# Applying a mixture-of-experts gate in ScalarE's PSUM eviction instead of in VectorE's combine

## The reference

```
x = x + 0.5 * ffn(layernorm(x))
x = x + attention(layernorm(x))          # score = q k^T / sqrt(hd), no softmax; rope on q and k
x = x + 0.5 * ffn(layernorm(x))

ffn(x):
    logits = x @ router_weight                        # 8 experts
    top_vals, top_idx = top_k(logits, 2)
    scores = softmax(top_vals)                        # the two gates of a token, their sum is 1
    w = zeros(T, 8) with scores at top_idx
    gate, up = even and odd columns of x @ gate_up_proj + bias, clipped at 7
    act  = (up + 1) * gate * sigmoid(1.702 * gate)
    down = act @ down_proj + bias
    out  = sum over experts of w * down
```

## Time and profile before

| | us |
|---|---|
| median of 3 runs | 793.53 (792.43 to 795.62) |
| the profiled execution, its own time | 793.87 |
| its span, first to last instruction | 792.0 |
| PE busy | 606.5 (77%) |
| VectorE busy | 496.9 (63%) |
| POOL busy | 418.2 (53%) |
| ScalarE busy | 312.1 (39%) |
| chain that ended last | PE 58%, VectorE 19%, DMA 7% |

### The profile page before, as it was taken

How to read it: one execution, slowest core, us unless ns; L and a number is a source line. 1 busy time by engine, 2 the same in 40 slices (tenths; PEclk the granted TensorE clock), 3 DMA queues, 4 the chain that set the end, 5 groups by cost and what they waited for, 6 DMA issues and landing times.

```text
span 792.0 us, 13509 instructions
## 1 busy us (share of the span) xinstructions
PE 606.5 (77%) x3716; PEld 511.5 (65%) x3725; DVE 496.9 (63%) x1103; ACT 312.1 (39%) x660; POOL 418.2 (53%) x484
## 2 busy tenths in 40 slices
PE   3656249999999995577777699924899999999800
PEld 2655138888888884355556589913688888888700
DVE  5855945555555552799998268875455555555367
ACT  3445234444444443244445224413444444444300
POOL 2655335777777754177777510002577777776400
PEclk9999999999999998699999779955899999999955
DMA  9566012333333321433331235200233233333189
GB/s 312 195 205 180 1 45 74 94 96 94 97 99 97 94 78 44 144 120 86 115 119 35 92 88 158 94 26 21 73 95 95 93 98 99 93 94 91 49 281 354
DMA packets 43366, 87.47 MB, mean 110 GB/s; under 512 B 7363, under 2 KB 22777, under 8 KB 42820
## 3 DMA queue, kind: packets, MB, share of 16 engines
q1 hardware_dynamic: 20898, 43.30, 16.9%
q0 software_dynamic: 13664, 35.35, 15.0%
q10 hardware_dynamic: 8770, 8.41, 3.1%
HBM read 53.50 MB, written 35.36 MB: 112 GB/s over the span
## 4 chain that ended last, share of the span: by engine, by line
PE 58%; DVE 19%; DMA 7%; issue 6%; POOL 5%; ACT 2%; DVEq 1%; SPq 1%; ACTq 0%; POOLq 0%
PE ps L770 14%; PE ps L771 14%; PE ps L772 14%; PE ps L761 10%; DVE xs L1264 5%; PE ps L765 3%; DMA work<-y_dram 2%; DVE work L1292 2%; DVE work L1291 2%; PE ps L788 2%; DMA xn_dram<-work 2%; POOL up_lo L435 2%; DVE work L1076 2%; DVE bst L1060 1%; DVE work L1192 1%
## 5 line engine op out<-in xcount | busy, mean ns | idle before, releaser
L761 PE MATMUL ps<-cst,work 128*128 128x128 f32 x824 | 137.1, 292 | 77.7 <-DVE work L1076 59.6
L474 POOL DMA_INDIRECT y_dram<-work,sidx x142 | 142.8, 1005 | 83.6 <-issue 49.5
L761 PEld LDWEIGHTS ps<-cst,work 128*128 128x128 f32 x824 | 103.9, 150 | 97.5 <-DVE work L1076 57.4
L466 POOL DMA_INDIRECT work<-xn_dram,gidx x142 | 139.3, 981 | 44.5 <-issue 44.5
L770 PE MATMUL ps<-up_hi,xT_hi 128*128 x284 | 125.6, 442 | 0.8 <-issue 0.8
L771 PE MATMUL ps<-up_lo,xT_hi 128*128 x284 | 113.2, 398 | 0.0
L772 PE MATMUL ps<-up_hi,xT_lo 128*128 x284 | 113.0, 398 | 0.0
L1214 DVE TENSOR_TENSOR xT_lo<-ps,xT_hi 128x512 fp32r<-128x512 f32 x72 | 49.8, 691 | 97.8 <-ACT xT_hi L613 97.8
L1229 DVE TENSOR_SCALAR work<-ps 128x256 f32<-128x256 f32 x142 | 60.3, 425 | 72.5 <-ACT work L627 72.5
L627 ACT ACTIVATE work<-ps 128x256 f32<-128x256 f32 x142 | 54.6, 384 | 111.4 <-PE ps L772 111.4
L635 ACT ACTIVATE work<-ps 128x512 f32<-128x512 f32 x72 | 42.6, 592 | 96.3 <-PE ps L772 96.3
(11 more groups left out here) (149 smaller groups left out, 1407.5 us busy)
## 6 DMA issues: line engine op xcount, KB each, us to landing
work<-y_dram SPq DMA_DIRECT2D x32, 512.0 KB, 3.9
xs<-L_attn_x SPq DMA_DIRECT2D x4, 1024.0 KB, 7.3
work<-L_ffn_gate_up_proj SPq DMA_DIRECT2D x8, 512.0 KB
q_dram<-work ACTq DMA_DIRECT2D x16, 256.0 KB, 3.0
work<-q_dram SPq DMA_DIRECT2D x16, 256.0 KB, 2.8
out<-xs SPq DMA_DIRECT2D x16, 256.0 KB, 5.6
xn_dram<-work SPq DMA_DIRECT2D x16, 255.0 KB, 4.5
xn_dram<-work ACTq DMA_DIRECT2D x16, 255.0 KB, 2.6
```

What stands on the lines that cost most here:

```text
L466: pool.indirect_dma_start(xg[:, k, u, 1:H], None, xn_dram[n], bass.IndirectOffsetOnAxis(ap=gidx[:, 2 * s + u:2 * s + u + 1], axis=0)).then ...
L474: pool.indirect_dma_start(y_dram[n], bass.IndirectOffsetOnAxis(ap=sidx[:, 2 * s + u:2 * s + u + 1], axis=0), ysb[:, k, u, :], None, bounds ...
L761: ins = nc.tensor.transpose(ps[:, bank, k:k + P], src[:, u, c * P:(c + 1) * P], ident)
```

## The change

The gate is no longer applied in `combine`. Where ScalarE moves a finished slot from PSUM to `ysb`, it now scales each row by the gate of that row (`y_out`), one instruction per slot instead of one per pair. The gate has to be known by slot, not by token: the first gate of each token is written to `xn_dram` as the 256th number of the token's row (4096 single numbers, by one DMA from ScalarE's queue), so that the gather brings it along. VectorE makes of it the scale of the slot's rows, with two tables made from the parity of `sidx`: for rank 0 half the gate, for rank 1 half of one minus the gate. `combine` becomes two plain additions of 512 numbers per partition. The second sigmoid and the halving are gone. POOL waits for the new DMA before the first gather, and its later gathers wait for `x_lo` instead of `x_T`. Rows of `xg` are 257 numbers long instead of 256.

```
-        xn_dram = [scratch(f"xn_dram{n}", [T, H - 1]) for n in range(2)]
+        xn_dram = [scratch(f"xn_dram{n}", [T, H]) for n in range(2)]
...
-        xg = area(0, RING, 2, H)
+        xg = area(0, RING, 2, H + 1)
...
# store_xn (SP, layer 0); xn_out (ScalarE's queue, layer 1) alike
-                sp.dma_start(pair(xn_v[0], g), xn_r[:, j % 2, :, 1:H]).then_inc(L[0].xn_stored[j % 2], 16)
+                sp.dma_start(pair(xn_v[0], g)[:, :, 0:H - 1], xn_r[:, j % 2, :, 1:H]).then_inc(L[0].xn_stored[j % 2], 16)
...
# experts, POOL
+                pool.wait_ge(l.gates_stored, 16)
                 pool.wait_ge(l.routed, 1)
...
-                        pool.indirect_dma_start(xg[:, k, u, 1:H], None, xn_dram[n],
+                        pool.indirect_dma_start(xg[:, k, u, 1:H + 1], None, xn_dram[n],
...
                     if s + RING < NP:
-                        pool.wait_ge(l.x_T, s + 1)
+                        pool.wait_ge(l.x_lo, s + 1)
                         gather(s + RING)
...
# gates, ScalarE
                 act.wait_ge(l.gap, 1)
-                nc.scalar.activation(gate[:, 1, :], small[:, 16:16 + NT], ACT.Sigmoid)
-                nc.scalar.activation(gate[:, 0, :], small[:, 16:16 + NT], ACT.Sigmoid, scale=-1.0).then_inc(l.gates, 1)
+                nc.scalar.activation(first_gate[:, :], small[:, 16:16 + NT], ACT.Sigmoid, scale=-1.0).then_inc(l.gated, 1)
+                act.wait_ge(l.gated, 1)
+                act.dma_start(xn_v[n][:, :, H - 1:H], first_gate[:, :, None],
+                              allow_slow_non_contiguous=True).then_inc(l.gates_stored, 16)
...
# y_out, ScalarE
                     act.wait_ge(l.y_ps, s + 1)
                     wait(act, l.scattered[k], 32 * rounds)
-                    n = halves(s)
-                    nc.scalar.activation(ysb[:, k, 0:n], ps[:, 7, :].rearrange("p (u h) -> p u h", u=2)[:, 0:n],
-                                         ACT.Copy).then_inc(l.y_sb, 1)
+                    act.wait_ge(l.x_lo, s + 1)
+                    for u in range(halves(s)):
+                        ins = nc.scalar.activation(ysb[:, k, u, :], ps[:, 7, u * H:(u + 1) * H], ACT.Copy,
+                                                   scale=slot_gate[:, k, u:u + 1])
+                    ins.then_inc(l.y_sb, 1)
...
# route, VectorE
-                dve.wait_ge(l.gates, 1)
-                st.done(v.tensor_scalar(gate[:, :, :], gate[:, :, :], 0.5, None, ALU.mult))
                 dve.wait_ge(l.names, 1)
                 v.engine_nop().then_inc(l.routed, 1)
+                st.done(v.tensor_single_scalar(parity[:, :], sidx[:, :], 1, ALU.bitwise_and))
+                st.done(v.tensor_copy(second[:, :], parity[:, :]))
+                st.done(v.tensor_scalar(sign[:, :], second[:, :], -1.0, 0.5, ALU.mult, ALU.add))
+                st.done(v.tensor_scalar(second[:, :], second[:, :], 0.5, None, ALU.mult))
...
# x_lo of the experts, VectorE
                     dve.wait_ge(l.x_hi, s + 1)
                     n = halves(s)
+                    for u in range(n):
+                        v.scalar_tensor_tensor(out=slot_gate[:, k, u:u + 1], in0=xg[:, k, u, H:H + 1],
+                                               scalar=sign[:, bass.ds(s * 2 + u, 1)],
+                                               in1=second[:, bass.ds(s * 2 + u, 1)], op0=ALU.mult, op1=ALU.add)
...
# combine, VectorE
                 def add(c):
-                    for u in range(2):
-                        xr = xs[:, bass.ds(g * 2 + u, 1), :].rearrange("p a h -> p (a h)")
-                        ins = v.scalar_tensor_tensor(out=xr, in0=ybuf[:, j, u, c, :],
-                                                     scalar=gate[:, c, bass.ds(g * 2 + u, 1)], in1=xr,
-                                                     op0=ALU.mult, op1=ALU.add)
-                    return ins
+                    return v.tensor_tensor(pair(xs, g), pair(xs, g), ybuf[:, j, :, c, :], ALU.add)
```

More of the change, by code:

```diff
@@ L171, in build @@
         logit = sb("logit", [P, NT, E], F32)
-        gate = sb("gate", [P, TOPK, NT], F32)
+        first_gate = sb("first_gate", [P, NT], F32)
+        sign = sb("sign", [P, NS], F32)
+        second = sb("second", [P, NS], F32)
+        parity = sb("parity", [P, NS], U32)
+        slot_gate = sb("slot_gate", [P, RING, 2], F32)
         gidx = sb("gidx", [P, NS], U32)
@@ L749, in _ @@
             logits_out(L[1], NG - 1, 1)
[L750 removed]
+            gates(1)
             experts(L[1])
@@ L1242, in activate, with step @@
                                            in1=upv[:, 0:n, :], op0=ALU.min, op1=ALU.mult).then_inc(l.act, 1)
-                x_lo(0, 0)
-                x_lo(1, 1)
+                x_lo(0, 0, 0)
+                x_lo(1, 1, 1)
                 activate(0, 0)
-                def body(it):
-                    for d in range(2):
-                        s, b = it * 2 + 1 + d, (1 + d) % 2
-                        x_lo(s + 1, 1 - b)
-                        activate(s, b, lambda: a_lo(s - 1, 1 - b))
-                st.loop(NP // 2 - 1, 2, body)
-                activate(NP - 1, 1, lambda: a_lo(NP - 2, 0))
+                def step(s, d):
+                    b = (1 + d) % 2
+                    if not (isinstance(s, int) and s + 1 >= NP):
+                        x_lo(s + 1, 1 - b, (d + 2) % RING)
+                    activate(s, b, lambda: a_lo(s - 1, 1 - b))
+                def body(it):
+                    for d in range(RING):
+                        step(it * RING + 1 + d, d)
+                st.loop((NP - 1) // RING, RING, body)
+                for s in range((NP - 1) // RING * RING + 1, NP):
+                    step(s, (s - 1) % RING)
                 a_lo(NP - 1, 1)
```

21 lines of the change are left out of this document (11 added, 10 removed).

## The result

The changed kernel takes 783.01 us (median of 4 runs, 781.41 to 783.10), beside 793.27 for the kernel before on the same chip (4 runs, 792.43 to 795.62): a ratio of 0.9861, 95% interval [0.9847, 0.9874]. The forecast was 785.3 us, faster. The profiled execution has a span of 781.2 us against 792.0.

The account below looks back on a forecast made before the run. PE was taken to bound the experts, VectorE the first attention pass, transfers the last stage; -8.5 - 0.6 + 0.8 + 0 = -8.3 us on 793.87 gives 785.6, stated as 785.3 because that execution lay above the median; range 780 to 797.

Parts of the forecast that it names:

- the +0.8 us of edges: Experts, both layers: later eviction +0.3, gate instructions +0.35, halving gone -0.25 per layer, 2 x (0.3 + 0.35 - 0.25).
- the second pair: First pass, combine instructions at 410.60, just before POOL's L504: merged into one, 1.17 to 0.68 us, 0.49 saved per group.
- three quarters: First pass: share taken of the 11 us (16 groups at 0.69 us), giving -8.5 us.
- the first pair: First pass, combine instructions at 413.62, running against four POOL instructions: 1.39 us before, only 0.20 us saving counted per group.
- the kept turn: First pass: one merged addition starting before POOL's instruction holds its turn, where two instructions lose one; part of 0.49 us.
- POOL's loop: First pass: POOL's instructions (5.6 us) and two hand-overs through ScalarE make 7.5 us per group, shortening only as VectorE's rotation does.
- the prediction's lower bound: First pass: surcharge from POOL stays, only the free part is saved, 0.20 us per pair, 32 x 0.20 = 6.4 us.
- only the first and the last combine are on the path: Last stage, DMA share 0.95: other combines' savings of 0.4 us each don't count; 0 to -1.5 us, taken as -0.6.
- The rival of the late store: Routing: the 4-byte-run store decides from 79 ns per run; at 120 ns 10.6 us late per layer, 806 us; chance 0.08.
- POOL in the experts: Rival: POOL, with 0.14 us per step to spare, becomes the bound through dearer gathers; 11 us more, 796; chance 0.07.
- The surcharge did not go: Rival, first pass: VectorE runs ahead of POOL and meets it less, up to 16 to 19 us saved, 778; chance 0.10.
- the turns eat all but a third of the 11 us: Rival: first pass held by POOL's instruction loop, only about a third of the saving arrives, 790 us; chance 0.15.

Follow-up runs that it names:

- gates alone: The change with the four-instruction combine put back and a gate of ones there; 793.92 us, ratio 0.9988 to the kernel before.

## Why the prediction was right, and where it was not

The total came out 2.3 us better than forecast, and its parts further off than that. In the profiled executions the gain is 10.8 us instead of 8.3: 1.0 less than forecast in the first pass, 1.3 more in the last stage, 1.3 in the first layer norm where nothing was forecast, and 0.85 because the +0.8 us of edges did not show.

**First pass, -8.5 forecast, -7.52 measured.** The sum came out near, but by another split. It credited 0.49 us to the second pair because one instruction would not lose its turn, 0.20 to the first, and took three quarters. In the changed timeline the groups differ, mostly as in the two below; the combine of rank 0 costs 0.67 to 0.69 us each time, and that of rank 1 either 0.68 or 1.04 (up to 1.23 in others):

```profile
399.66 0.67 DVE L1284 TENSOR_TENSOR xs<-xs,work 128x512 f32<-128x512 f32 x1
...
402.29 1.47 DVE L1087 TENSOR_SCALAR work<-xs,sbmv,small 128x256 f32<-128x256 f32 x2
403.68 1.04 DVE L1284 TENSOR_TENSOR xs<-xs,work 128x512 f32<-128x512 f32 x1
...
406.58 0.67 DVE L1284 TENSOR_TENSOR xs<-xs,work 128x512 f32<-128x512 f32 x1
...
410.20 0.72 DVE L1087 TENSOR_SCALAR work<-xs,sbmv,small 128x256 f32<-128x256 f32 x2
410.85 0.68 DVE L1284 TENSOR_TENSOR xs<-xs,work 128x512 f32<-128x512 f32 x1
```

So the first pair went from 1.39 to 0.67 us, far more than the 0.20 allowed for it, and the normalisation gives some of it back (1.47 instead of 0.72). What remains is best read by group. The forecast's sum was 0.69 us a group: 0.40 for the prices without POOL and 0.29 for one turn kept. The old combine takes 7.44 us a group and the new one 6.91, which is 0.53. The prices without POOL account for 0.38 of it (0.87 - 0.68, twice), so of the kept turn about 0.15 arrived; this is an estimate, since kernels with the same combine differ by 0.06 to 0.12 us in this mean. The three-quarters factor, for which the prediction gave another reason, POOL's loop, hid that: 0.75 x 0.69 is 0.52. That the stage came out near is in part luck. The stages say the same less sharply: the three kernels with one plain addition per pair and POOL's work as it was average 124.9 us, the three with the old combine 132.3, which is 7.4 us against 6.4 (the prediction's lower bound) or 6.1 (by the rows above).

The step that failed is the kept turn, 0.29 of the 0.49 us, counted in full: by that estimate about half of it came, and the rest of what POOL costs VectorE was passed on to the next instructions. The rule of the exclusive lock (the Trainium skill, SBUF — State Buffer, who interferes with whom) pointed to the lower bound, as the prediction said; the measurement lies halfway between it and the full 0.69. That the number of POOL's instructions sets the loss, as the prediction read it, does not hold: with four instead of eight a group takes 6.87 us, and 6.95 with VectorE's rotation merged as well, against 6.91. What does set it stays open.

**Last stage, -0.6 forecast (0 to -1.5), -1.92 measured.** The failed step is "only the first and the last combine are on the path". Four groups are loaded ahead, so the first four combines run back to back at VectorE's pace before the transfers become the limit. SP's queue shows it, before and after: the first releases come 1.70 us apart, then 1.33.

```profile
760.65 0.34 SPq L397 DMA_DIRECT2D work<-y_dram  x1
...
762.34 0.34 SPq L397 DMA_DIRECT2D work<-y_dram  x1
...
764.05 0.34 SPq L397 DMA_DIRECT2D work<-y_dram  x1
```
```profile
751.40 0.34 SPq L402 DMA_DIRECT2D work<-y_dram  x1
...
752.72 0.34 SPq L402 DMA_DIRECT2D work<-y_dram  x1
...
754.04 0.34 SPq L402 DMA_DIRECT2D work<-y_dram  x1
```

Four times 0.37 are 1.5 us. Counted from the first combine, the eleventh release is still 1.50 us earlier than before, the twelfth 1.88, and the end of the last combine 1.98. So the first four rounds bring 1.5 us; where the other 0.4 arises can't be told from one execution of each.

**First layer norm, nothing forecast, -1.31 measured.** The prediction asked what the wider rows do to the gathers, and not what they do to the stores. The trace of before had the row: 1.3 us of VectorE's idle time ended by the store to `xn_dram`.

**Edges and covers.** ScalarE's pair of evictions was taken at 0.9 us and costs 2 x 0.471 = 0.94, of which the surcharge for the scale column is 471 - 384 = 87 ns, in the bound of at most 0.13. VectorE's gate instructions take 224 ns each instead of 158, 66 ns more; they have a column as scalar operand too, which cost 61 ns in the combine. Both are covered, as forecast: PE is busy in all 183 us, and leaving out the extra evictions, or adding all gate work without the additions, changes nothing that can be measured. The +0.8 us of edges can't be told from the scatter; experts and routings together came out 0.1 us shorter.

**The store.** It was costed at nothing, because its bounds of 2.6 and 14 us both lay under the cover of 22.7; it lands in 7.1. The rival of the late store (79 ns per run) falls: even if all above the 2.2 us of an ordinary landing were the runs' own, (7.1 - 2.2) / 256 = 19 ns each. The rule that speaks against it (the Trainium skill, DMA: Bandwidth & Descriptors, rules for kernel authors: one descriptor per element) agrees with the trace in kind: the queue counts 8224 packets more, about one per number, and the 16 KB take three times as long to land as 255 KB. No run here shows the reading and modifying under 512 bytes. At this size the store fits in the routing's shadow.

**The other rivals.** POOL in the experts kept its idle 0.46 us before the first scatter and its step. The surcharge did not go: the stage gained 7.5 us, not 16 to 19. That the turns eat all but a third of the 11 us did not come true either, though in the mechanism it had half of the kept turn right.

## What to carry to other kernels

Cost an edit on VectorE beside a busy GpSimd at its price without GpSimd, and look for what seems to be saved beyond that in the neighbouring instructions: here about half of it was passed on to them. One group of a timeline can mislead, since who is held up changes from group to group; read the mean time of many groups. Dropping a per-partition scalar operand was worth about as much in this stage as halving the number of instructions (3.9 and 3.7 us). In a stage that transfers bound, count how many buffers are filled ahead: those first rounds run at the engine's pace, and the engine's saving counts once for each.

## What the runs showed of the hardware that was not expected

- A store of the same 255 numbers per row lands in 2.2 us on ScalarE's queue in all eleven kernels whose rows lie 256 numbers apart in DRAM, and in 2.6 to 2.8 in the three whose rows lie 255 apart. On SP's queue it is 3.9 to 4.2 us in ten of the eleven and 4.6 in gates alone, against 4.5 to 5.0 in the three. Which property of the address counts was not tried.
- 4096 runs of 4 bytes are issued in 0.6 us, hardly more than 256 runs of 2 KB, and land in 7.1.
- A per-partition scalar operand costs VectorE 61 ns in an instruction of 256 numbers (482 against 421 ns).
- A normalisation of VectorE, which reads one tile and two columns, is held up by POOL like an addition of two tiles: up to 2.61 us instead of 0.72 for a pair.
- GpSimd's low parts, 3.1 us per group, cost the first pass 20 to 25 us in the 14 groups where they were left out, 1.4 to 1.8 us per group (an estimate from one execution of each kernel), though VectorE and not GpSimd was the busiest engine.
